# More constant products of TensorE in the pauses at the openings of five stages

## The reference

```python
x = x + _L0_xattn_ref(_layernorm(x), ctx, itok, ...)      # attention over a window of ctx       (L0x)
x = x + _L0_ffn_ref(_layernorm(x), ...)                   # conv + causal attention, 4 experts   (L0f, L0m)
x = x + _L1_xattn_ref(_layernorm(x), ctx, ctx, ...)       # cross attention, 16 heads            (L1x)
x = x + _L1_ffn_ref(_layernorm(x), ...)                   # tree of 256 leaves                   (L1f)
x = x + _L2_xattn_ref(_layernorm(x), ctx, ctx, ...)       # cross attention, 16 heads            (L2x)
x = x + _L2_ffn_ref(_layernorm(x), ...)                   # latent causal attention, 8 + 1 experts (L2f, L2m)
x = x + _L3_xattn_ref(_layernorm(x), ctx, ctx, ...)       # softmax over the heads               (L3x)
x = x + _L3_ffn_ref(_layernorm(x), ...)                   # int8 product                         (out)
```

## Time and profile before

| | |
|---|---|
| median of 3 runs | 1636.36 us (1632.52 to 1644.97) |
| profiled execution | 1630.4 us, span 1628.7 us |
| PE busy | 1406.0 us (86%) |
| DVE, ACT, POOL busy | 987.6 us (61%), 687.7 us (42%), 628.2 us (39%) |
| mean granted TensorE clock | 0.916 |

### The profile page before, as it was taken

One profiled execution on the slowest core, in us unless ns is written; L12 is line 12 of the kernel. 1 busy time (PEld: TensorE's weight loads), 2 busy tenths in 40 slices (PEclk: granted clock), 3 DMA queues, 4 the chain that ended last, 5 costly groups with the idle time before them and its releaser, 6 DMA issues. The chain is left out here.

```text
span 1628.7 us, 23696 instructions
## 1 busy us (share of the span) xinstructions
PE 1406.0 (86%) x9145; PEld 715.1 (44%) x9145; DVE 987.6 (61%) x1770; ACT 687.7 (42%) x1204; POOL 628.2 (39%) x626
## 2 busy tenths in 40 slices
PE   7868786988989999899868999899999877889984
PEld 3345443433334444444334444454445433355542
DVE  4898939777742211468566773745556344588866
ACT  2444432766742000257534774244434432355522
POOL 2487734354223221333124312533421312356762
PEclk8889997989999999879987998999999978999996
DMA  5000010000020000100001002000000010000000
GB/s 111 0 1 0 1 48 1 1 1 1 1 82 1 1 0 0 53 1 1 11 0 54 2 2 47 1 2 1 2 1 2 2 31 1 7 1 2 2 1 28
DMA packets 17382, 20.65 MB, mean 13 GB/s; under 512 B 7835, under 2 KB 13195, under 8 KB 16760
## 3 DMA queue, kind: packets, MB, share of 16 engines
q1 hardware_dynamic: 15440, 17.33, 3.6%
q10 hardware_dynamic: 1832, 1.80, 0.5%
HBM read 17.94 MB, written 1.05 MB: 12 GB/s over the span
## 5 line engine op out<-in xcount | busy, mean ns | idle before, releaser
L1852 DVE CUSTOM_DVE_ANT_0 P<-P,L2f_mask 128x128 f32<-128x128 f32 (+3 forms) x256 | 118.5, 521 | 99.9 <-PE P L1744 99.9
L1029 DVE TENSOR_REDUCE L0f_nm<-P 128x2 f32<-128x768 f32 (+3 forms) x88 | 97.5, 1120 | 38.1 <-PE P L926 37.9
L2028 PE MATMUL P<-L0m_hm,L0m_w 128*128 128x512 f32 x256 | 112.2, 597 | 0.0
L1822 ACT ACTIVATE L2f_prob<-P 128x1024 f32<-128x1024 f32 x80 | 80.6, 1025 | 73.1 <-PE P L1756 73.1
L1663 POOL TENSOR_SCALAR_AFFINE_SELECT L2f_prob<-L2f_prob 128x512 f32<-128x512 f32 x64 | 39.9, 638 | 161.4 <-ACT L2f_prob L1822 161.4
L983 ACT ACTIVATE L0f_prob<-P 128x512 f32<-128x512 f32 x160 | 86.9, 610 | 33.8 <-PE P L937 32.5
L1744 PE MATMUL P<-L2f_ks,L2f_qs 48*128 48x512 f32 (+3 forms) x512 | 90.9, 467 | 0.3 <-DVE L2f_nm L1852 0.3
L1756 PE MATMUL P<-L2f_qs,L2f_ks 49*128 49x256 f32 (+3 forms) x512 | 84.5, 444 | 3.1 <-DVE L2f_nm L1852 2.3
L2431 POOL TENSOR_TENSOR L3x_exm<-L3x_exm,L3x_rec 128x2048 f32<-128x2048 f32 x16 | 72.4, 4530 | 24.1 <-DVE L3x_rec L2617 24.1
L1306 PE MATMUL P<-ident,L0x_pv 128*128 128x128 f32 x384 | 53.7, 305 | 27.1 <-POOL L0x_pv L1207 27.1
L880 POOL TENSOR_SCALAR_AFFINE_SELECT L0f_prob<-L0f_prob 128x512 f32<-128x512 f32 x64 | 39.9, 638 | 95.2 <-ACT L0f_prob L983 88.3
(11 more groups left out here) (578 smaller groups left out, 3329.5 us busy)
## 6 DMA issues: line engine op xcount, KB each, us to landing
L0m_w<-in_L0m_w SPq DMA_DIRECT2D x1, 2048.0 KB, 8.0
L0f_va<-in_L0f_va SPq DMA_DIRECT2D x3, 512.0 KB, 5.3
L0x_prod<-in_x SPq DMA_DIRECT2D x2, 512.0 KB, 5.9
L0x_segi<-in_segb SPq DMA_DIRECT2D x1, 1024.0 KB, 18.2
L0m_w<-in_L0m_w SPq DMA_DIRECT2D x1, 1024.0 KB, 10.0
out<-out_o SPq DMA_DIRECT2D x4, 256.0 KB, 2.4
L1x_va<-in_va SPq DMA_DIRECT2D x3, 256.0 KB, 3.1
L1x_vr<-in_vr SPq DMA_DIRECT2D x3, 256.0 KB, 4.1
```

Source lines behind the costliest of these rows:

```text
L1029: nc.vector.tensor_reduce(S.nm[:, qt, first:first + 2 * many].rearrange("p (i e) -> p e i", e=2), P[:, bank:bank + 2, 0:many * width].rear ...
L1822: nc.scalar.activation(S.prob_of(b, g)[:, at:at + 2, :], P[:, bank:bank + 2, :], ACT.Exp).then_inc(*S.act_done.up())
L1852: m = nc.vector.tensor_tensor_reduce(out=at, in0=at, in1=mask[:, T - width:T], scale=1.0, scalar=-3.0e38, op0=ALU.add, op1=ALU.max, accum_ ...
L2028: m = mm(P[:, slot(b, i) + part, :], w1[:, e, part * 512 + i * 128:part * 512 + i * 128 + 128], hm[b % 2][:, e, :], start=e == 0, stop=e = ...
```

## The change

The change raises the count of constant products at four places and adds seven calls. Per place: L0f `t1` 28 to 44, `t2` new 22; L1x and L2x (one function) `t1` 16 to 29, `t2` new 8; L2f `t1` 22 to 35, `t2` new 9; L0m 9 ahead of `lg` 0 and 8 ahead of `lg` 2; L2m 16 ahead of `var` 0, 12 ahead of `lg` 2, 24 ahead of the second `turn`. These are 171 products more. In `turn` the wait for the bank now stands ahead of the wait for the choice.

```diff
@@ phase_cross (L1x and L2x)
                     if s == ("t1", 0, 0):
-                        keep_busy(nc, G, 6, 16)
+                        keep_busy(nc, G, 6, 29)
                     pe.wait_ge(S.qx_ready.sem, b + 1)
                     S.turn_q(pe, s)
                 elif kind == "t2":
+                    if s == ("t2", 0, 0):
+                        keep_busy(nc, G, 6, 8)
                     pe.wait_ge(S.nx_ready.sem, 2 * b + n // 2 + 1)
@@ phase_conv_attention (L0f)
-                        keep_busy(nc, G, 6, 28)
+                        keep_busy(nc, G, 6, 44)
...
+                    if s == ("t2", 0, 0):
+                        keep_busy(nc, G, 6, 22)
@@ phase_latent_heads (L2f)
-                        keep_busy(nc, G, 6, 22)
+                        keep_busy(nc, G, 6, 35)
...
+                    if s == ("t2", 0, 0):
+                        keep_busy(nc, G, 6, 9)
@@ phase_experts
                 elif kind == "var":
+                    if b == 0 and not one:
+                        keep_busy(nc, G, 0, 16)
                     pe.wait_ge(*(sq_pool if b % 2 else sq_dve).at(0, b // 2 + 1))
...
                 elif kind == "lg":
                     if b == 0:
+                        if one:
+                            keep_busy(nc, G, 6, 9)
                         pe.wait_ge(ld.sem, 16 * len(early))
+                    elif b == 2:
+                        keep_busy(nc, G, 0 if one else 6, 8 if one else 12)
                     pe.wait_ge(z_ready.sem, b + 1)
...
                 elif kind == "turn":
-                    pe.wait_ge(hot_up.sem, b + 1)
                     if b:
                         pe.wait_ge(turned.sem, 1)
+                        if not one:
+                            keep_busy(nc, G, 6, 24)
+                    pe.wait_ge(hot_up.sem, b + 1)
```

## The result

| | before | after |
|---|---|---|
| median of 4 runs each, taken in turns | 1636.76 us (1632.52 to 1644.97) | 1618.30 us (1615.31 to 1621.24) |
| profiled execution, span | 1630.4 us, 1628.7 us | 1617.4 us, 1615.6 us |
| PE busy, mean granted clock | 1406.0 us, 0.916 | 1426.1 us, 0.934 |

The ratio is 0.9881, with a 95% interval of 0.9838 to 0.9924: 1.2% faster, 12 to 27 us on the 1636.76 of before. 1619 us were forecast. TensorE is busy 20 us longer and the program is 13 us shorter in the two profiled executions. Where this came from differs from the forecast place by place. In a later measurement of the changed kernel (e10_again) one execution took 2034.6 us at a mean clock of 0.636; it is left out of the ratio given there.

A forecast was written before the change was run, and what follows sets the result against it. TensorE, the busiest engine, bounds the work behind its pauses, where its clock is down. Terms 0.5 + 3.5 + 6 + 2 + 2.5 + 4.4 = 18.9 us, less 1.5 for chance, off 1636.4: 1619 us; range 1605 to 1633.

The forecast's parts named there:

- the chances: Whole kernel: faster by over 1% 0.46, the same 0.50, slower by over 1% 0.04.
- the signs that the forecast named: Clock at 1.00 behind pauses, L1x's second stretch 12 us, ScalarE's 5.58 us wait under 3, L0m's experts 3 to 4 us earlier.
- L0f, second pause: L0f `t2`: constants start at the lower clock, late unless it rises soon; transposes and first rounds behind get faster, 0.5 us.
- L0m, to its first output product: L0m: variances 1.9 us less, router products 0.95, scaling and next router products 0.7; sum 3.5 us.
- L1x, VectorE's split of the queries to that of the maxima: Behind L1x `t1`: 1.7 us on the unbroken TensorE work and 0.6 us on the remaining rounds, 2.3 us.
- L1x, first and second stretch: Behind L1x `t2`: first stretch 10.6 us plus lateness, second like its twin at 1.00; gains 1.9 + 3.1 us.
- L2x, VectorE's split of the queries to that of the maxima: Behind L2x `t1`: 2.1 us less 0.6 us for late constants, 1.5 us.
- L2x, first and second stretch: Behind L2x `t2`: first stretch 10.6 us plus lateness, gaining 0.6 us.
- L2f, second pause: Behind L2f `t2`: 24 round products at the upper clock and following busy work gain 2.5 us; low end 0.
- L2m: Three pauses: variances, logits and part of the gates 1.4 us; later logits 0.9; turn and gates 2.1; sum 4.4 us.
- that rival: Clock falls again right behind the pauses, L1x and L2x losing the gain from `t2` on: about 10 us, 1628 us; chance 0.22.
- The rule on transposes: Trainium skill: full clock does not engage for transposes, so L1x and L2x lose 2.3 + 1.5 us; 1621 us, chance 0.04.

The follow-up runs named there:

- e10_again: The changed kernel itself measured once more, nothing altered: 1617.0 us, ratio 0.9891 to the kernel before.
- e3_thin: The changed kernel with each of the 171 added products on 32 rows and 32 columns of the array, counts kept: 1643.8 us, ratio 1.006 to before.
- e1_experts: The kernel before with only the added constants of the expert stages (L0m and L2m): 1633.6 us, ratio 0.9977 to before.
- e9_pool: e4_short with GpSimd's first multiplication in L0m waiting for VectorE's second choice of experts: a single run of 1614.1 us.
- e4_short: The changed kernel with fewer constants: cross attentions' `t2` 8 to 4, L0f `t2` 22 to 14, L2m's first pause 16 to 12: 1613.1 us, ratio 0.9866.
- e11_all: e8_units with GpSimd's wait of e9_pool and 10 instead of 14 constants in L0f's second pause: 1609.1 us, ratio 0.9803 to before.
- e6_fill: e4_short with constants in more pauses: ahead of two rounds in L1x and L2x, two masks in L2m, L0m's second turn: 1610.6 us, ratio 0.9856.
- e2_attn: The kernel before with only the added constants of the attentions (L0f, L1x, L2x, L2f): 1618.5 us, ratio 0.9899 to before.
- e7_turning: e4_short with transposes of the identity instead of constants in L1x and L2x, 96 for 29 and 14 for 4: 1614.4 us, ratio 0.9856.
- e8_units: e6_fill with three more constants ahead of the first unit of L1x and L2x: 1609.8 us, ratio 0.9853 to before.

## Why the prediction was right, step by step

The mechanism was right: where the clock was up behind a pause the stages gained, and where it stayed down they did not (e3_thin). The forecast of 1619 us was met, and the measured ratio's interval lies on both sides of 1%, as the chances did. That it was met to 1 us is luck, since several terms are off and offset each other, and some of what the profiles miss is open. Of the signs that the forecast named, L1x's second stretch of 12 us and the clock over the first transposes came in all three traces with its constants (in L2x the clock fell there in one); but ScalarE's wait in L0m fell to 3.81 us and not under 3, L0m gained 1.2 us and not 3 to 4, and one sign of being wrong came too, constants at 0.45 us each in L1x's second pause. Measured in the three traces that have the constants in question (in this order: the changed kernel, the one of the two parts that has them, the changed kernel again), against the trace of before:

| term | forecast | measured, us gained |
|---|---|---|
| L0f, second pause | 0.5 (-2 to 2) | -2.4, -3.2, -3.1 |
| L0m, to its first output product | 3.5 (1.9 to 5) | 1.2, 1.2, 1.3 |
| L1x, VectorE's split of the queries to that of the maxima | 2.3 | 2.5, 1.2, 2.4 |
| L1x, first and second stretch | 5.0, less 1.5 for chance | 2.3, 4.4, 3.9 |
| L2x, VectorE's split of the queries to that of the maxima | 1.5 | 0.7, 2.7, 0.6 |
| L2x, first and second stretch | 0.6 | -0.2, 0.8, 0.2 |
| L2f, second pause | 2.5 (0 to 3.4) | 2.7, 2.7, 2.7 |
| L2m | 4.4 (-0.9 to 10) | 7.0, 3.5, 5.5 |

The measured values add up to 13.8, 13.3 and 13.5 us, against 18.9 us forecast (for L1x and L2x the forecast took 6 and 2 us of the terms shown, and it took 1.5 us off the sum for chance); the medians differ by 18.5 us, with an interval from 12 to 27 us. The rest of some 5 us is open. It is in the attentions: alone they give 1.0%, some 17 us, of which their trace shows 8.6. It may lie in the profile of before, which ran 6 us below its median, at a mean clock of 0.916 (the median of 13 later executions is 0.912): without the attentions' constants the profiled runs were faster than the medians by 6 us (before) and 11 us (e1_experts), with them they lay between 5 us faster and 7 us slower. That would mean that these two traces show less than the usual loss in the attentions; no run shows where.

**The step that failed: L0f.** "Late unless the clock rises soon" was right, and it did rise, after 3.2 us. But the row ended 0.9 to 1.7 us late, and the forecast had the work behind it faster, with no second fall of the clock. It fell again in all three traces with 22 constants, for 6.8 us each time, and the first stretch got 2.4 to 3.2 us longer, outside the range given. The two costs can be told apart: 14 constants were never late, and the stretch took 22.27 us in five kernels, in which the clock stayed up, and 24.82 us in e9_pool, where it fell for 6.8 us. So the second fall cost 2.5 us, and the lateness came on top in full (24.82 + 0.9 = 25.7 us, measured 25.69). What made the clock fall again is not shown. A row that starts at the lower level has to be counted with that level.

**The cross attentions' second pause** was priced as if the clock held up to it: eight constants late by 0.3 and 0.7 us, a first stretch of 10.6 us. The forecast named the short rounds in between as the reason why it may fall and gave that rival 0.22, but took only 1.3 us off L1x for it. It fell in both stages of all three traces (in L1x of the first, 0.50 from 696.8 on, the row took 3.6 us), and TensorE came 1.1 to 2.2 us late. The value of 10.6 us itself was right to 0.6 us, as e4_short (10.60, 10.21) and e11_all (10.0) show, with half as many constants or with more waits filled; L2x also had 11.75 and 11.94 us with rows as short. The 1.5 us taken off for chance stand, as 15.2 us came in three of six cases without full-size constants in `t2`; but one of the three was in L2x, whose second stretch the forecast had put at nothing.

**L2x's first pause** was counted as 0.6 us late. Its row began 8.9 us ahead of the transposes (5.9 before) and ended 1.3 to 3.0 us ahead of VectorE's split. In the two traces with the longest wait left the clock fell during the transposes (at 870.8 in the first), and 0.7 and 0.6 us came instead of 1.5; in the third it held up to 872.3, and 2.7 us came.

**L0m** was read too high by 2.3 us. The routers, at 2.14 and 2.18 us, wait for VectorE's second scaling. The variances ran at the upper level for a part only in the first trace, and wholly, in 1.96 us, in the two others, so that the masks were 2.5 and 3.7 us earlier. Of this VectorE lost 1.2 us, since GpSimd's multiplication, starting earlier, now met two of its small instructions instead of one. And where 2.5 us were left at the first gate products, these met more of the lower level, which lasted up to 25 us behind VectorE's first row as before: sixteen took 9.3 and 9.4 us instead of 8.2. So 1.2 to 1.3 us remained each time. With these products at 1.00 (e6_fill) the first output product is 2.5 us earlier than before, and with the wait of e9_pool as well (e11_all) 3.9 us. VectorE's loss was a wait that the change moved under other work, and the trace of before had shown its sign in one row, a cast of 1.14 us among others of 0.19.

**L2m** was within its range, though built up wrongly. From the third logits to the first gates behind the masks 1.9 to 2.0 us came instead of 0.9, in all three traces, as the clock held through logits and turn and fell only at the masks, and 0.5 to 0.9 us more up to the second turn. The third place brought 0.7 instead of 2.1 us: the turn took 0.62 instead of 1.03 us, but the gates 3.34 instead of 3.41 us, since the clock fell at 1338.5 in the masks' waits. The first place scattered (3.5, 0.4, 1.8) around the 1.4 taken. Against e2_attn instead of before all three values of the table are 1.6 us smaller.

L2f and L0f's first pause (nothing gained) came as forecast, and so did L1x's first pause in two traces of three; in e2_attn its row ended 1.0 us late. The price of 0.22 us at the upper level, and its double at the lower, held: 0.43 us in e3_thin's 22. The rule on transposes was given 0.04, and e7_turning went against it.

## What to carry to other kernels

A constant product in a pause is worth what stands behind it at the lower clock and is waited for; count the row at the level that TensorE has when it begins, and make it so short that it fits even then. Where the engine does short products at another engine's pace, put a few constants into the waits instead of a long row at the end: with constants in the first pause and none up to the second, the clock had fallen ahead of the transposes of `t2` in all fourteen cases (L1x and L2x in the seven traces of such kernels), and with waits in between filled as well (e6_fill, e8_units, e11_all) in one of six. A clock that falls ahead of work on which TensorE is the bound can stay down for long (13.6 us in e6_fill), and that costs more than the wait. A gain on one engine should be followed to the next one that it sets off, as GpSimd's earlier start took 1.2 us of VectorE's choice in L0m.

## What the runs showed of the hardware

- Products on 32 rows and 32 columns left the granted clock at 0.50 through 9.56 us of a busy TensorE in L0f, where products of the same length on the full array had it at 1.00 after 3.2 us; in L2f, where it was at 1.00 when they began, it stayed there through 2.11 us of them.
- Ninety-six transposes ran for 5.52 us at 1.00 and the next sixteen, in 1.07 us, as well.
- The clock can stay at 0.50 under unbroken work: 13.6 us in L1x of e6_fill, with units, values and projections; the same code stayed at 1.00 where it began there.
- Small instructions of VectorE (128 x 32) took 1.16 us instead of 0.19 beside GpSimd's multiplications of 128 x 512, and 0.19 us again when GpSimd started later.
